# Who makes the low halves of eight experts' weights, and when, between attention and a mixture of experts

## The reference

```python
def attn(x, g1, b1, Wq, Wkv, Wo, g2, b2):
    xn = layernorm(x) * g1 + b1
    q, (k, v) = xn @ Wq, split(xn @ Wkv)          # 16 heads of 64; one k and one v
    out = softmax(q @ k.T * 64 ** -0.5) @ v
    return layernorm(out @ Wo) * g2 + b2

def experts(h, gate_w, gate_up_w, down_w):
    probs = softmax(h @ gate_w.T)
    topw, sel = top_k(probs, 2); topw /= sum(topw)
    gu = einsum("th,efh->etf", h, gate_up_w)      # 8 experts, 1024 columns: gate 512, up 512
    hact = gu[..., 512:] * gelu(gu[..., :512])
    return sum_over_e(weight * (hact @ down_w))   # weight: topw where e was chosen, else 0

x = x + attn(layernorm(x), ...)
x = x + experts(layernorm(x), ...)
```

## Time and profile before

| | |
|---|---|
| median of 3 runs | 629.05 us (627.08 to 629.2) |
| profiled execution | 631.12 us, its span 629.1 us |
| mean granted TensorE clock | 0.97 of full speed |
| busy | PE 580.3 us (92%), DVE 427.6 (68%), ACT 304.0 (48%), POOL 389.4 (62%) |
| second block's first instruction | about 470.3 us into the span |

### The profile page before, as it was taken

One profiled execution on the slowest core, in us unless ns is written; L12 is line 12 of the kernel. 1 busy time (PEld: TensorE's weight loads), 2 busy tenths in 40 slices (PEclk: granted clock), 3 DMA queues, 4 the chain that ended last, 5 costly groups with the idle time before them and its releaser, 6 DMA issues. The chain is left out here.

```text
span 629.1 us, 8805 instructions
## 1 busy us (share of the span) xinstructions
PE 580.3 (92%) x2608; PEld 330.5 (53%) x2608; DVE 427.6 (68%) x815; ACT 304.0 (48%) x570; POOL 389.4 (62%) x320
## 2 busy tenths in 40 slices
PE   7899999999999998989999988999987698999980
PEld 5555454444554453445545434454423477888970
DVE  3876658559746978784686889866678768444433
ACT  3245645356446554444655445365437264555530
POOL 5357667567669855688796569869648234354330
PEclk9999999999999999889999999999998799999995
DMA  5111011011010100070000000000007000230005
GB/s 174 68 69 70 24 46 68 1 68 39 32 69 0 70 2 1 4 284 15 2 1 2 2 5 19 13 2 1 10 4 206 23 22 26 67 93 27 25 10 200
DMA packets 23980, 29.28 MB, mean 47 GB/s; under 512 B 4403, under 2 KB 14901, under 8 KB 23936
## 3 DMA queue, kind: packets, MB, share of 16 engines
q1 hardware_dynamic: 21664, 24.50, 11.9%
q0 software_dynamic: 2272, 4.24, 2.0%
HBM read 13.73 MB, written 15.32 MB: 46 GB/s over the span
## 5 line engine op out<-in xcount | busy, mean ns | idle before, releaser
L1077 ACT ACTIVATE prob<-s_ps 128x512 f32<-128x512 f32 x256 | 150.6, 598 | 184.1 <-PE s_ps L1182 182.2
L1003 DVE TENSOR_REDUCE rowmax<-max_ps 128x1 f32<-128x512 f32 x256 | 173.2, 686 | 82.7 <-PE max_ps L1151 80.7
L940 POOL TENSOR_TENSOR fold<-prob 128x1024 f32<-128x1024 f32 x63 | 149.7, 2376 | 92.8 <-ACT prob L1077 92.3
L1196 PE MATMUL pv_ps<-prob,v 128*64 128x512 f32 x512 | 138.8, 622 | 0.0
L1180 PE MATMUL s_ps<-q_hl,khh 128*128 128x512 f32 x256 | 118.1, 461 | 1.0 <-ACT prob L1077 0.6
L1151 PE MATMUL max_ps<-khh,q_hl 128*128 128x512 f32 x256 | 103.5, 410 | 6.2 <-DVE q_hl L992 3.0
L1182 PE MATMUL s_ps<-q_hm,kly 65*128 65x512 f32 x256 | 102.1, 399 | 0.0
L1180 PEld LDWEIGHTS s_ps<-q_hl,khh 128*128 128x128 f32 x256 | 48.7, 190 | 79.6 <-ACT prob L1077 60.9
L946 POOL TENSOR_TENSOR psums<-fold 128x512 f32<-128x512 f32 x63 | 81.7, 1297 | 4.9
L1151 PEld LDWEIGHTS max_ps<-khh,q_hl 128*128 128x128 f32 x256 | 49.3, 193 | 26.2 <-DVE rowmax L1003 9.6
L1182 PEld LDWEIGHTS s_ps<-q_hm,kly 65*128 65x128 f32 x256 | 48.8, 191 | 9.0 <-issue 3.3
(11 more groups left out here) (221 smaller groups left out, 793.2 us busy)
## 6 DMA issues: line engine op xcount, KB each, us to landing
sorted_rows<-raw_w SPq DMA_DIRECT2D x36, 260.0 KB, 2.6
raw_w<-in_gate_upT SPq DMA_DIRECT2D x8, 512.0 KB, 7.9
wd<-in_downT SPq DMA_DIRECT2D x8, 256.0 KB, 3.9
raw_w<-parts SPq DMA_DIRECT2D x8, 256.0 KB, 4.4
psums<-sorted_rows SPq DMA_DIRECT2D x22, 65.0 KB, 1.8
x<-in_x SPq DMA_DIRECT2D x4, 256.0 KB, 5.6
out<-x SPq DMA_DIRECT2D x4, 256.0 KB, 2.8
xs_first<-sorted_rows SPq DMA_DIRECT2D x15, 65.0 KB, 1.9
```

What stands on the lines that cost most here:

```text
L940: nc.gpsimd.tensor_tensor(fold[:, :, :], prob[:, head % 4, 0:2, :], prob[:, head % 4, 2:4, :], ALU.add).then_inc(prob_folded, 1)
L1003: nc.vector.tensor_reduce(rowmax[:, group % 2, it, i:i + 1], max_ps[:, k % 2, :], AX_X, ALU.max).then_inc(max_done, 1)
L1077: nc.scalar.activation(prob[:, head % 4, jt, :], s_ps[:, k % 2, :], ACT.Exp, scale=SCALE).then_inc(exp_done, 1)
L1196: last = nc.tensor.matmul(pv_ps[DH * hd:DH * hd + DH, :], v[:, b % 2, jt, :], prob[:, head % 4, jt, :], start=(jt == 0), stop=(jt == JT - 1))
```

## The change

VectorE makes the low parts of experts 0, 1 and 2: the first ahead of `hidden(0)`, the second behind it, the third behind NORM 0. It makes no others. GpSimd makes those of experts 3 to 7, each in one operation of 1024 columns, behind its row sends and behind a new wait for VectorE's three. ScalarE makes the high parts of experts 0 and 1 ahead of `x_high(1)`; the others shift accordingly. The counts in TensorE's waits before tile 6 follow.

```diff
-            def low_gate_up(eng, e, done, pieces=1):
-
+            VECTOR_LOW = 3
+
+            def low_gate_up(eng, e, done):
                 eng.wait_ge(wh_ready, e + 1)
-                for n in range(pieces):
-                    cols = slice(e * GU + n * GU // pieces, e * GU + (n + 1) * GU // pieces)
-                    last = eng.tensor_tensor(wl[:, cols], raw_w[:, cols], wh[:, cols].bitcast(F32), ALU.subtract)
-                last.then_inc(done, 1)
+                cols = slice(e * GU, (e + 1) * GU)
+                eng.tensor_tensor(wl[:, cols], raw_w[:, cols], wh[:, cols].bitcast(F32), ALU.subtract).then_inc(done, 1)
...
-                for e in range(2, E - 2):
-                    low_gate_up(pool, e, wl_pool, 2)
+
+                pool.wait_ge(wl_ready, VECTOR_LOW)
+                for e in range(VECTOR_LOW, E):
+                    low_gate_up(pool, e, wl_pool)
...
                 tail_vector(dve, "RSPLIT", last_unit, 0)
+                low_gate_up(dve, 0, wl_ready)
                 hidden(0)
+                low_gate_up(dve, 1, wl_ready)
                 tail_vector(dve, "NORM", last_unit, 0)
-                low_gate_up(dve, 0, wl_ready)
+                low_gate_up(dve, 2, wl_ready)
                 tail_vector(dve, "NORM", last_unit, 1)
                 hidden(1)
                 tail_vector(dve, "NORM", last_unit, 2)
-                low_gate_up(dve, 1, wl_ready)
                 tail_vector(dve, "NORM", last_unit, 3)
                 hidden(2)
-                low_gate_up(dve, E - 2, wl_ready)
-                low_gate_up(dve, E - 1, wl_ready)
...
                 nc.scalar.activation(spare[:, :], ones[:, 0:1], ACT.Gelu)
+                high_weights(0)
+                high_weights(1)
                 x_high(1)
                 gelu(0)
-                high_weights(0)
-                high_weights(1)
+                high_weights(2)
                 gelu(1)
                 x_high(2)
-                high_weights(2)
                 high_weights(3)
+                high_weights(4)
                 take_turned(0)
                 gelu(2)
-                for e in range(4, E):
+                for e in range(5, E):
                     high_weights(e)
...
-                            pe.wait_ge(wl_ready, 4)
-                            pe.wait_ge(wl_pool, E - 4)
+                            pe.wait_ge(wl_ready, VECTOR_LOW)
+                            pe.wait_ge(wl_pool, E - VECTOR_LOW)
```

## The result

| | before | changed |
|---|---|---|
| median (runs) | 630.24 us (20) | 624.38 us (20) |
| lowest to highest | 625.95 to 635.05 | 619.58 to 629.13 |
| profiled execution, its span | 631.12, 629.1 | 625.64, 623.7 |
| from the second block's first instruction to the end | 158.8 | 151.05 |

The ratio is 0.9931 [0.9906, 0.9957], a gain of 4.3 us (2.7 to 5.9); the two medians lie further apart, 5.9 us, at the edge of that interval. Runs over 1.5% above the fastest of their kernel are left out of the ratios and, further down, of the gains; with them the changed kernel's gains in the experiments would be 7.2, 4.9 and 5.5 instead of 6.0, 4.1 and 4.6. The forecast was 9.3 us, to 619.8. The sign was right and the stall went as forecast; the size of the gain was not right.

The account below looks back on a forecast made before the run. TensorE, busy 92% of the span, was taken to pace the kernel. Gains of 7.71 + 1.77 + 0.35 = 9.83 us, less 0.5, gave 9.3: from a median of 629.05 to 619.8 us, range 618.0 to 622.3.

Parts of the forecast that it names:

- the stall: TensorE's idle time ahead of OUT 3, waiting for NORM 3 behind a held VectorE low part: all 7.71 us go.
- The half clock behind it: OUT 3, the turn and `down` after TensorE's idle time return to the full clock: 1.77 us gained.
- ScalarE's order: Two high parts moved ahead of `x_high(1)` at no cost, freeing `x_high(2)`: 0.35 us gained, between 0 and 0.48.
- The row's length: GpSimd's five whole subtractions take 11.85 us from 481.05, ending between 492.90 and 493.4; 492.9 taken.
- VectorE's three low parts: In the second block's early tiles, 1.22 us each, with GpSimd's row sends running beside them: cost nothing.
- The hold of `var_eps`: VectorE's `var_eps`, due at 492.28, waits for GpSimd's last subtraction until 492.9: 0.6 us.
- the term of 0.5: TensorE's `down(2)` comes late through `weigh(1)` after held `var_eps`: 0.5 us given back, between 0 and 1.1.
- A: Rival: nothing holds `var_eps`, or GpSimd's row ends earlier; gain 9.83 us, to 619.2 us; chance 0.17.
- C: Rival: low clock stays in part, having another cause than idle time; gain 8.1 us, to 621.0 us; chance 0.06.
- B: Rival: GpSimd's row is longer, to 493.4 or beyond; gain 8.8 to 8.3 us, 620.3 to 620.8; chance 0.20.
- D: Rival: the long low part has another cause than GpSimd's row, so the stall stays; 629 us; chance 0.03.
- E: Rival: whole-operation row also holds VectorE with one PSUM input, delaying NORM 1 or 2; 631.0 us; chance 0.03.

Follow-up runs that it names:

- Q: The changed kernel, with the whole change made to P; median 624.38 us, ratio 0.9931 to P.
- P: The kernel before the change; median 630.24 us.
- e0: Q once more with no edit, in the first group of runs; median 624.85 us, ratio 0.9885 to P.
- e2: Q with ScalarE's old order: high parts of experts 0 and 1 behind the gelu of tile 0; median 625.70 us, ratio 0.9901 to P.
- e1: Q with VectorE's first two low parts subtracting from a PSUM bank instead of SBUF (values wrong, for times alone); median 625.37 us, ratio 0.9895 to P.
- e5: P once more with no edit, one run for a second profile; last `weigh` 139.47 us behind the block's start, no median.
- e8: P with GpSimd waiting for VectorE's first two low parts before its own; median 626.81 us, ratio 0.9965 to P.
- v5: Q with five row sends ahead of GpSimd's row, three behind the norm's first power, first result's send behind the second; 622.02 us, ratio 0.9903 to P.

## Why the prediction was wrong in size

**Right.** GpSimd's row kept VectorE's low part out, and the stall went whole, 7.71. The half clock behind it went, about 1.77. Together with 0.37 from ahead of OUT 3 that made 9.85 at tile 3 against 9.83. The last agreement is in part luck: Q's block began at a lower clock than P's (its first gate product took 2.03 against 1.75), and where both kernels begin at the full clock ScalarE's order alone is worth 0.85 (e0 and e2), not 0.35. The row's length was 11.70 against 11.85. `var_eps` came when forecast and was held to the row's end.

**The step that failed** is in *VectorE's three low parts*: "GpSimd's row sends run beside all three ... The cost is nothing", and with it "The row starts at 481.05 as before". I had read whether a send slowed VectorE (1.22 at 478.93) and not whether VectorE slowed a send. That one low part started 0.14 behind a send's own start (478.79) and could not show it. In Q three low parts start ahead of a send and hold it, 2.6 us in all at the row's start (1.9 where the block begins at the full clock, and there `var_eps` comes 0.7 earlier too). The hold of `var_eps` became 3.0 instead of 0.6, and in place of the term of 0.5 `down(2)` idled 2.9. e1 shows the cause alone: with an input in PSUM the row starts at 10.75 and `var_eps` is held 0.6. So of 9.3 predicted, 7.2 were there by the last tile.

**The second failure** is the base. I took one profile of P for the kernel. P has another course, seen in e5, 2.6 us shorter (3.2 in e8), in which the stall that I removed does not exist and another of 5.62 does. Q's last `weigh` is at 134.90 and 134.91 with either clock at its start, by the chance that the half clock behind `down(2)` takes back what the faster start gives. So Q gains 7.2 on the one course and 4.0 to 4.6 on the other. The timed gains, 4.3 (2.7 to 5.9) and 4.9 on average in the three groups, lie between the two. How many of P's runs take which course is not known.

**The rivals.** A (no hold) and C (low clock stays) are excluded by the 3.15 and by the clock of 1.00 from 492 to 497, where OUT 3 is long past, and from 485 to 492. B had the right place and the wrong cause: the row did end late, because it started late, not because it was longer. D and E are excluded by the low parts' 1.22 and by NORM 1's and 2's 0.68 and 0.69 (the row began behind NORM 3 there, so E's own condition did not arise in Q; in v5 it did: NORM 2 and 3 took 0.69 at 480.75 and 482.28, beside whole operations from 479.58). Undoing ScalarE's part costs nothing in the end (e2). One reading of the earlier trace rows was too simple: at 270 us VectorE's instruction starts at 269.98, 0.29 ahead of the fold that it is said to have waited for, so the order of the recorded starts does not by itself say who waits for whom.

**The range** (618.0 to 622.3; measured 624.38) took the hold of `var_eps` as at most 1.1, from the row's length alone. I had bounded the length of the row from both sides and its start not at all.

## What to carry to other kernels

When two engines exclude each other, read the trace in both directions: which of the two began first, and whether the other's instructions, sends included, grew. A send that happened to begin first shows no cost, and does not prove that there is none. Put an instruction that reads two SBUF tensors ahead of another engine's long row, never inside it, and look at more than one profile of the kernel before: where two queues arrive within a microsecond or two of one another, chance in the clock can decide the order, and the stall seen may be one of several.

## What the runs showed of the hardware

- A VectorE subtraction of two SBUF tensors holds an indirect DMA's issue on GpSimd that starts behind it: 1.95 instead of 0.97, ending 0.84 to 0.86 behind it. With one input in PSUM there is no hold (0.97). The Trainium skill ("SBUF — State Buffer", "Who interferes with whom") says that a DMA stalled by a VectorE operation is one whose descriptors GpSimd makes. The trace agrees as far as it is the issue on GpSimd's queue that grew. The same section tells of a probe in which `tensor_tensor` did not stall DMA; here it did.
- In these runs the hold of VectorE lasts as long as GpSimd goes on back to back (a low part took 9.65 beside eight halves, 12.28 beside five wholes), and it catches an operation of 128x4 elements with one input as well (0.17 becomes 3.15, and 3.90 beside ten halves). The Trainium skill, in the same section, states the hold for one instruction.
- The granted clock varied between executions of one kernel. 0.01 of its mean went with 4.9 us, more than Q gained at one clock, 3.0 to 3.6. Behind an idle time of 2.9 us it was 0.66 in one profile of Q and 1.00 in another.
